# A graph layer on one core: 200 instead of 192 binned groups, summed in blocks of 32, 16 and 8

## The chip, the cores and the metric

The kernel runs on one core of a Trainium2 chip. The metric is the device time in microseconds (us), from the first to the last instruction of the core. Engines: TensorE (PE), VectorE (DVE), ScalarE (ACT), GpSimd (POOL), and SyncE (SP), which issues most transfers.

## What is computed

A layer of a graph network over 6250 nodes and 206,250 edges; `dst` is sorted, `src` is not.

```python
h = maximum(layernorm(x), 0)                       # 6250 x 64
m = relu(concat([h[dst], edge_attr]) @ W1.T + b1)  # 206250 x 128
m = relu(m @ W2.T + b2)                            # 206250 x 128
agg = segment_sum(m, src) / maximum(count(src), 1) # 6250 x 128
z = relu(concat([h, agg, u]) @ Wa.T + ba)
out = x + z @ Wb.T + bb                            # 6250 x 64
```

## The kernel before, in words

**Tiling.** The edges go through in 403 groups of 512 (four tiles of 128). All five engines run the same software pipeline of steps s = 0, 1, 2, ...; each engine has its own instruction stream in the order of the code, and semaphores tie them. For group s the first layer is one float32 product of 512 columns (two instructions, L1373); a window of 64 table rows stands for `h[dst] @ W1`, since `dst` is sorted. ACT evacuates it with relu (L923), PE multiplies by W2 one step later (L1399, 8 instructions for four tiles), ACT evacuates that (L943).

**Two ways to sum by `src`.** A *plain* group is summed within each tile by a mask product (L1389), copied by ACT (L931) into one of four buffers `scat`, and added to four tables in DRAM by four indirect transfers of GpSimd (L821, one for each tile). DVE makes the mask (L1182) and the row numbers (L1187, L1190). ACT has to wait until the transfers from a buffer have landed before it fills it again, so PE can run ahead of GpSimd by four plain groups at most.

A *binned* group (every odd group from 3 to 385, 192 in all) needs no scatter of its own. Node n belongs to bin n % 49: 49 bins of 128 nodes. DVE ranks each row within its bin (L1154 to L1163, after a product with `prefix`, L1417) and makes a permutation with 4 places in each of 49 bins and 60 places for overflow. PE permutes the four tiles (L1350, 16 instructions), ACT copies them (L906, four copies of 128x260), and SP stores them to `slots` in DRAM (L606, L607). The 60 overflow rows of the four tiles are added by DVE (L1204, L1205) into `vpre`; SP copies `vpre` of each group into one half of `V` (L615), two groups fill one `V`, and PE makes of V's key column a row (L1410), DVE a mask, PE a sum (L1423), and GpSimd one scatter for each pair of groups (L809).

**Blocks and units.** When the 32 binned groups of a block are in `slots`, the block is summed in 25 *units* of two bins (the last has one). For a unit SP issues two loads (L629), each 128 rows (32 groups x 4 places) of 520 floats (4 tiles x 130). DVE compares the keys with 128 node numbers (L1215, 8 one-hots for a unit), PE multiplies (L1361, 16 instructions), DVE adds the result to `acc` (L1134; L1131 copies for the first block). Three units fit in the ring of buffers `BR`.

`unit_steps` writes the order by hand. The 25 units of a block are spread over the steps until the next block is complete, always on even steps: one unit in about 2.56 steps, 0.78 a pair of steps (0.83 for the fifth block, 60 steps). The last block starts 5 steps after its last group, group 385. From group 386 on all groups are plain, and the units of the last block go beside them, two in a step after the third.

**SP's stream** in each step: the edge block (L579, every second step), the `dst` rows (L587, every fourth), the row number of the window and its load (L592, L593), the `src` rows (L599), then for a group six steps back the two stores (L606, L607), for one seven steps back the copy to V (L615), then the loads of the step's unit. The copy is issued in the step after the one in which PE wants it in the program's count, so SP runs ahead of PE.

**The end.** After the last load SP waits for all scatters and reads the four tables (L645, L641); DVE adds them and `acc` (L1231 to L1234), ACT scales, PE transposes and multiplies by Wa and Wb, in 13 chunks.

A *pair* below is two steps, one plain and one binned group: 4 + 1/2 scatters. The lines that set the share of binned groups and the order of the units:

```python
LAST_SORTED = 386
def is_sorted(g): return 2 < g < LAST_SORTED and g % 2 == 1
firsts = [block[-1] + VREAD + 2 for block in BLOCKS[:-1]] + [BLOCKS[-1][-1] + TAIL_LAG]
s = firsts[k] + 2 * (span * q // (2 * UNITS))
```

Of the kernel before, what the change touches and what calls it, by code (L numbers as in the profile page):

```python
# [47 lines left out]
LAST_SORTED = 386  # L48
# [16 lines left out]
ROUNDS = [[(0, 4), (4, 5)]] + [[(a, a + 4), (a + 4, a + 8)] for a in range(5, 45, 8)] + [[(45, 49)]]  # L65
# [26 lines left out]
BLOCKS = [BINNED[k:k + BLOCK] for k in range(0, NH, BLOCK)]  # L92
# [42 lines left out]
def unit_steps():  # L135
    at = {}
    firsts = [block[-1] + VREAD + 2 for block in BLOCKS[:-1]] + [BLOCKS[-1][-1] + TAIL_LAG]
    for k in range(len(BLOCKS) - 1):
        for q in range(UNITS):
            span = firsts[k + 1] - firsts[k]  # L140
            s = firsts[k] + 2 * (span * q // (2 * UNITS))
            at.setdefault(s, []).append((k, q))
    alone = VSUM - TAIL_LAG
    for q in range(UNITS):
        s = firsts[-1] + (q if q < alone else alone + (q - alone) // 2)
        at.setdefault(s, []).append((len(BLOCKS) - 1, q))
    return at
# [3 lines left out]
STEPS = max(max(UNITS_AT) + TAIL_LEAD + 1, NG + VSUM + 1)  # L151
# [32 lines left out]
def arrived(m):  # L184
    parts = {n: unit_bins(q)[1] for (_, q), n in UNIT_NO.items()}
    return sum(parts[n] for n in users(m))


# [1338 lines left out]
```

## Time and profile before

| what | value |
|---|---|
| median of 3 timed runs | 1929.52 us (1921.0 to 1935.98) |
| span of the profiled execution | 1917.2 us |
| PE busy | 1737.8 us (91%) |
| GpSimd busy | 1528.8 us (80%) |
| ACT busy | 1433.6 us (75%) |
| DVE busy | 1289.0 us (67%) |
| PE weight loads busy | 1470.5 us (77%) |
| TensorE clock granted, mean | 0.972 of full speed |
| DMA traffic, mean | 194 GB/s |

The profiled execution gives the span from the first to the last instruction, and its times are those of one execution; the timed runs are executions without the profiler. SP computes nothing, so it has no busy time on the page: its issues and waits stand in the timeline and in a view of waits of their own. "Issue" ahead of an instruction is idle time for which the profile shows no other engine.

### The profile page before, as it was taken

What the parts mean: (1) busy time and instruction counts of PE and PEld (TensorE: products, weight loads), DVE (VectorE), ACT (ScalarE), POOL (GpSimd) and SP (SyncE); (2) the same over time, 40 slices, a digit from 0 to 9 for tenths busy, and PEclk for the clock granted to TensorE, in tenths of its full rate; (3) what the DMA queues carried; (4) which work ended last, traced back from release to release, by engine and by line L of the source; (5) the groups of instructions that cost most, each with busy time, mean ns of one, the idle gap of its engine ahead of it and who ended that gap; (6) DMA issues with size and microseconds to landing.
All of it is one profiled execution on the core that took longest, in us unless ns stands there. A gap on an engine that the chain in (4) does not pass through costs nothing.

```text
span 1917.2 us, 43265 instructions
## 1 busy us (share of the span) xinstructions
PE 1737.8 (91%) x12472; PEld 1470.5 (77%) x12472; DVE 1289.0 (67%) x4235; ACT 1433.6 (75%) x2975; POOL 1528.8 (80%) x991
## 2 busy tenths in 40 slices
PE   6898888999999999999999999999999999978837
PEld 4677666888888888888788788888888888867725
DVE  8565555667767676777776777777776676756727
ACT  4788887878888877788788787878877877862306
POOL 8488888888888888888888888888888888888850
PEclk8999999999999999999999999999999999998969
DMA  9988888999999999999999999999999999999856
GB/s 329 269 166 151 151 151 149 187 198 193 198 192 192 201 190 196 201 192 192 200 197 187 185 199 198 200 193 197 204 194 198 191 199 199 197 183 234 176 116 217
DMA packets 319400, 372.10 MB, mean 194 GB/s; under 512 B 42272, under 2 KB 203264, under 8 KB 318528
## 3 DMA queue, kind: packets, MB, share of 16 engines
q1 hardware_dynamic: 182400, 305.12, 55.6%
q0 software_dynamic: 135360, 62.15, 34.4%
q8 instruction: 110, 1.80, 0.4%
q10 hardware_dynamic: 1408, 2.03, 0.3%
q14 instruction: 122, 1.00, 0.1%
HBM read 203.87 MB, written 159.27 MB: 189 GB/s over the span
## 4 chain that ended last, share of the span: by engine, by line
POOL 44%; issue 19%; PE 17%; DMA 11%; DVE 5%; ACT 3%; SPq 1%; ACTq 0%; POOLq 0%; DVEq 0%
POOL sums L821 39%; DMA sums<-regA,idx 7%; POOL sums L809 5%; PE bank L1361 4%; PE bank L1350 4%; PE bank L1399 3%; PE bank L1373 3%; DVE regC L1215 2%; PE bank L1389 1%; DMA regC<-slots 1%; DMA regA<-sums 1%; DMA sums<-vscat,vidx 1%; ACT regA L931 1%; DVE regC L1182 1%; PE bank L1275 1%
## 5 line engine op out<-in xcount | busy, mean ns | idle before, releaser
L821 POOL DMA_INDIRECT sums<-regA,idx x844 | 1333.9, 1580 | 291.7 <-issue 244.4
L1350 PEld LDWEIGHTS bank<-h,regC 128*128 128x128 f32 x3072 | 389.0, 194 | 183.1 <-ACT h L943 134.0
L1350 PE MATMUL bank<-h,regC 128*128 128x130 f32 x3072 | 421.7, 281 | 63.0 <-ACT h L943 62.8
L1373 PE MATMUL bank<-regA,L 128*128 128x512 f32 x806 | 435.8, 623 | 4.6 <-DVE regA L1147 3.0
L1399 PE MATMUL bank<-w,h 128*128 128x128 f32 x3224 | 431.3, 277 | 0.0
L923 ACT ACTIVATE h<-bank,b1c 128x512 f32<-128x512 f32 x403 | 275.7, 684 | 198.0 <-PE bank L1373 193.1
L1399 PEld LDWEIGHTS bank<-w,h 128*128 128x128 f32 x3224 | 398.0, 194 | 1.1 <-ACT h L923 0.6
L1215 DVE TENSOR_SCALAR regC<-lows,regC 128x128 f32<-128x128 f32 x1176 | 257.7, 315 | 147.6 <-DMA regC<-slots 124.0
L1361 PE MATMUL bank<-regC 128*128 128x129 f32 x2352 | 298.3, 281 | 34.4 <-issue 19.0
L943 ACT ACTIVATE h<-bank 128x512 f32<-128x512 f32 x403 | 240.9, 598 | 111.1 <-PE bank L1399 107.2
L1361 PEld LDWEIGHTS bank<-regC 128*128 128x128 f32 x2352 | 277.2, 193 | 41.8 <-issue 38.1
L1389 PEld LDWEIGHTS bank<-h,regC 128*128 128x128 f32 x1688 | 223.1, 192 | 102.2 <-issue 98.7
L906 ACT ACTIVATE regC<-bank 128x260 f32<-128x260 f32 x768 | 270.4, 385 | 4.5 <-PE bank L1350 3.9
L912 ACT ACTIVATE bank<-b2b 128x512 f32<-128x512 f32 x403 | 242.4, 602 | 11.2
L1389 PE MATMUL bank<-h,regC 128*128 128x130 f32 x1688 | 224.7, 276 | 0.5 <-ACT h L943 0.5
L1182 DVE TENSOR_TENSOR regC<-src,srcF 128x512 f32<-128x512 uint16 x211 | 146.4, 694 | 99.7 <-DMA src<-rows_src 95.1
L1156 DVE TENSOR_TENSOR regC<-bank,ranks 128x784 f32<-128x784 f32 x192 | 184.5, 961 | 0.0
L931 ACT ACTIVATE regA<-bank 128x520 f32<-128x520 f32 x211 | 126.4, 599 | 71.7 <-DMA sums<-regA,idx 54.6
L809 POOL DMA_INDIRECT sums<-vscat,vidx x96 | 153.0, 1594 | 31.2 <-issue 26.8
L1154 DVE TENSOR_REDUCE rank<-bank 128x4 f32<-128x196 f32 x192 | 68.3, 356 | 140.0 <-PE bank L1417 137.6
L1140 DVE TENSOR_TENSOR regC<-bank,overs 128x240 f32<-128x240 f32 x192 | 77.0, 401 | 115.8 <-PE bank L1434 114.9
L954 ACT ACTIVATE regA<-dstR,oh_bias 64x512 f32<-64x512 uint8 x192 | 137.6, 717 | 4.9
(142 smaller groups left out, 1540.3 us busy)
## 6 DMA issues: line engine op xcount, KB each, us to landing
regC<-slots SPq DMA_DIRECT2D x294, 260.0 KB, 5.6
regA<-in_ea SPq DMA_DIRECT2D x202, 256.0 KB
slots<-regC SPq DMA_DIRECT2D x192, 260.0 KB
src<-rows_src SPq DMA_DIRECT2D x107, 256.0 KB
slots<-regC SPq DMA_DIRECT2D x192, 138.1 KB
sums<-regA,idx POOLq DMA_INDIRECT x844
dstR<-rows_dst SPq DMA_DIRECT2D x101, 128.0 KB
sums<-zeros SPq DMA_DIRECT2D x20, 645.0 KB, 7.0
```

The costliest lines, as they stand in the source:

```text
L809: nc.gpsimd.indirect_dma_start(out=sums[k], out_offset=bass.IndirectOffsetOnAxis(ap=vidx[:, j % 6:j % 6 + 1], axis=0), in_=vscat[:, j % 4, ...
L821: nc.gpsimd.indirect_dma_start(out=sums[k], out_offset=bass.IndirectOffsetOnAxis(ap=idx[:, n % RING, t:t + 1], axis=0), in_=scat[:, n % 4, ...
L906: nc.scalar.activation(slot_sb[:, n % 2, :, t, :], psSlot(t), ACT.Copy).then_inc(slot_ready, 1)
L912: nc.scalar.activation(psL2(g % 2).rearrange("p (t f) -> p t f", t=TPG), b2b[:, :].unsqueeze(1).broadcast_to([P, TPG, H]), ACT.Copy).then_ ...
L923: nc.scalar.activation(h1[:, s % 2, :], psL1(s % 2), ACT.Relu, bias=b1c[:, :]).then_inc(h1_ready, 1)
L943: nc.scalar.activation(h2[:, g % 2, :, 0:H], psL2(g % 2).rearrange("p (t f) -> p t f", t=TPG), ACT.Relu).then_inc(h2_ready, 1)
L1215: made = VE.tensor_scalar(oh2[0:rows, m % 2, i, t, :], lows[0:rows, i, :], loaded(m)[0:rows, i, t, C:W], -float(b), ALU.subtract, ALU.is_e ...
L1350: last = T.matmul(psSlot(t)[:, k, :], place, h2[:, g % 2, t, :], start=True, stop=True)
L1361: last = T.matmul(psUnit(m)[:, i * C:(i + 1) * C], oh2[0:rows, m % 2, i, t, :] if not general else zeros[0:rows, 0:LO], loaded(m)[0:rows, ...
L1373: T.matmul(psL1(s % 2), L[:, s % RING, :], R[:, s % RING, :], start=True, stop=True).then_inc(l1_done, 1)
L1389: last = T.matmul(bank[:, 6 + t // 2, (t % 2) * W:(t % 2 + 1) * W], S[:, n % 4, t, :], h2[:, g % 2, t, :], start=True, stop=True)
L1399: last = T.matmul(psL2(g % 2)[:, t * H:(t + 1) * H], h1[:, g % 2, t * TILE:(t + 1) * TILE], w2[:, :], start=False, stop=True, skip_group_c ...
```

## The change

- Every odd group from 3 to 401 is binned: 200 binned groups and 203 plain ones (before 192 and 211).
- The blocks have 32, 32, 32, 32, 16, 16, 16, 16 and 8 groups. For a block of 16 or 8 a load puts two or four times as many rows on the partitions, each with two tiles or one tile of the four (`FOLD` 2 or 4): it still fills 128 partitions, with rows of 260 or 130 floats. A unit then has 4 or 2 one-hots instead of 8, and 8 or 4 matmul instructions instead of 16; it still has two loads and one addition.
- The units of blocks 0 to 2 are spread as before. From block 3 on they stand as soon as the schedule allows: every second step for block 3 (steps 266 to 315), one in each step for blocks 4 to 7 (316 to 415), two in a step for block 8 (416 to 428). The last step that has a group is 402.
- The ring `BR` is counted in quarters: three units of block 3, six of blocks 4 to 7 or twelve of block 8 fit. The three spare buffers of the last block are gone. From step 405 on the units' sums go through four banks of PSUM.
- DVE writes the overflow of the first group of a pair straight into V; SP copies only the second (one copy a pair of groups).
- V's key row is made by PE's transpose instead of a product with the identity.
- ACT copies the permuted tiles in pairs: two copies of 128x520 a group.
- The count of overflows at the start covers 800 tile columns instead of 784, with one part more.

```diff
-LAST_SORTED = 386
+FIRST_SORTED, LAST_SORTED = 3, 402
-BLOCK = 32
+SIZES = [32] * 4 + [16] * 4 + [8]
-ROUNDS = [[(0, 4), (4, 5)]] + [[(a, a + 4), (a + 4, a + 8)] for a in range(5, 45, 8)] + [[(45, 49)]]
+ROUNDS = [[(0, 4), (4, 5)]] + [[(a, a + 4), (a + 4, a + 8)] for a in range(5, 45, 8)] + [[(45, 49), (49, 50)]]
-UNIT_RING, SPARE = 3, 3
-TAIL_LAG, TAIL_LEAD = 5, 1
+UNIT_RING = 3
+LATE, LATE_LAG, STEADY = 2, 5, 3
-BLOCKS = [BINNED[k:k + BLOCK] for k in range(0, NH, BLOCK)]
+BLOCKS = [BINNED[sum(SIZES[:k]):sum(SIZES[:k + 1])] for k in range(len(SIZES))]
+FOLD = [max(SIZES) // len(block) for block in BLOCKS]
 def unit_steps():
...
+    due = 4 * firsts[STEADY]
+    for k in range(STEADY, len(BLOCKS)):
+        due = max(due, 4 * firsts[k])
+        for q in range(UNITS):
+            at.setdefault(due // 4, []).append((k, q))
+            due += 8 // FOLD[k]
...
-            return bank[:, 0 if m >= PAIRED and m % 2 else 1, 0:PAIR * C]
+            return bank[:, 1 if m < ALONE else 2 + (m - ALONE) % 4, 0:PAIR * C]
...
-                if is_sorted(s - VREAD):
-                    n = BINNED_NO[s - VREAD]
-                    j, half = n // 2, n % 2
-                    sp.wait_ge(vpre_ready, n + 1)
-                    if half == 0:
-                        wait(sp, vsum_done, j - 1)
-                        wait(sp, vidx_ready, j - 1)
-                    sp.dma_start(V[half * OVER:(half + 1) * OVER, j % 2, :], vpre[:, half, :]).then_inc(v_in[n % 4], 16)
+                if closes(s - VREAD):
+                    j = BINNED_NO[s - VREAD] // 2
+                    sp.wait_ge(vpre_ready, 2 * j + 2)
+                    sp.dma_start(V[OVER:2 * OVER, j % 2, :], vpre[:, :]).then_inc(v_in[j % 2], 16)
...
-                    if buffer_of(m) >= UNIT_RING:
-                        sp.wait_ge(vpre_ready, NH)
-                    if len(users(m)) > 1:
-                        sp.wait_ge(unit_done, users(m)[-2] + 1)
-                    h0 = BINNED_NO[block[0]]
+                    wait(sp, unit_done, UNIT_FREED[m])
+                    h0, n = BINNED_NO[block[0]], len(block)
+                    folded = slots.rearrange("n p (f x) -> n (p f) x", f=FOLD[k])
+                    rows = CAP * FOLD[k]
                     for i in range(nb):
-                        sp.dma_start(loaded(m)[0:CAP * len(block), i, :, :].rearrange("p t c -> p (t c)"),
-                                     slots[h0:h0 + len(block), CAP * (b + i):CAP * (b + i + 1), :]).then_inc(unit_in[buffer_of(m)], 16)
+                        sp.dma_start(loaded(m)[0:rows * n, i, :, :].rearrange("p t c -> p (t c)"),
+                                     folded[h0:h0 + n, rows * (b + i):rows * (b + i + 1), :]).then_inc(unit_in[UNIT_AT[m]], 16)
...
-                nc.scalar.activation(slot_sb[:, n % 2, :, t, :], psSlot(t), ACT.Copy).then_inc(slot_ready, 1)
+                nc.scalar.activation(slot_sb[:, n % 2, :, t:t + 2, :].rearrange("p h t c -> p t h c"), psSlots, ACT.Copy).then_inc(slot_ready, 1)
...
-                    if n >= 2:
-                        dve.wait_ge(v_in[(n - 2) % 4], 16 * ((n - 2) // 4 + 1))
+                    j, half = n // 2, n % 2
+                    if half == 0:
+                        wait(dve, vsum_done, j - 1)
+                        wait(dve, vidx_ready, j - 1)
+                    elif j >= 1:
+                        dve.wait_ge(v_in[(j - 1) % 2], 16 * ((j - 1) // 2 + 1))
...
-                    VE.tensor_tensor(vpre[:, n % 2, :], vhalf[:, 0, :], vhalf[:, 1, :], ALU.add).then_inc(vpre_ready, 1)
+                    VE.tensor_tensor(V[0:OVER, j % 2, :] if half == 0 else vpre[:, :], vhalf[:, 0, :], vhalf[:, 1, :], ALU.add).then_inc(vpre_ready, 1)
...
-                        for t in range(TPG):
+                        for t in range(size):
...
-                if t >= 2:
-                    pe.wait_ge(slot_ready, TPG * n + t - 1)
+                if t == 2:
+                    pe.wait_ge(slot_ready, 2 * n + 1)
...
-                    T.matmul(psVrow, V[:, j % 2, C:W].broadcast_to([P, P]), ident[:, :], start=True, stop=True).then_inc(vrow_done, 1)
+                    T.transpose(psVrow, V[:, j % 2, C:W].broadcast_to([P, P]), ident[:, :]).then_inc(vrow_done, 1)
```

SP's stream in a late pair of steps, where the fifth block was summed before and a block of 16 is now. `p_table` is the window's load, `V<-vpre` the copy, `regC<-slots` the loads of a unit, `slots<-regC` the stores. Before:

```order
L593 DMA L<-p_table 64x128
L615 DMA V<-vpre 60x130
L629 DMA regC<-slots 128x1x520 x2
L592 TENSOR_LOAD base
L592 ISA x2
L593 ISA
L593 DMA L<-p_table 64x128
L606 DMA slots<-regC 68x520
L607 DMA slots<-regC 128x520
L579 DMA regA<-in_ea 64x1024
```

And now:

```order
L605 DMA L<-p_table 64x128
L611 DMA src<-rows_src 128x1024
L623 DMA V<-vpre 60x130
L636 DMA regC<-slots 128x1x260 x2
L604 TENSOR_LOAD base
L604 ISA x2
L605 ISA
L605 DMA L<-p_table 64x128
L618 DMA slots<-regC 68x520
L619 DMA slots<-regC 128x520
L636 DMA regC<-slots 128x1x260 x2
L591 DMA regA<-in_ea 64x1024
```

Each of the two steps has a unit's two loads now, with rows half as long, and the copy to V stands in every second pair only.

SP's stream at the end, from the last window's load to the reads of the tables (`regA<-sums`). Before:

```order
L593 DMA L<-p_table 64x128
L629 DMA regC<-slots 128x1x520 x11
L645 DMA regA<-sums 128x516 x4
L641 DMA regA<-sums 128x1032 x16
```

And now:

```order
L618 DMA slots<-regC 68x520
L619 DMA slots<-regC 128x520
L636 DMA regC<-slots 128x1x260 x2
L623 DMA V<-vpre 60x130
L636 DMA regC<-slots 128x1x260 x17
L636 DMA regC<-slots 128x1x130 x49
L652 DMA regA<-sums 128x516 x4
L648 DMA regA<-sums 128x1032 x16
```

After the last window's load 11 loads were left; now 78 are (10 more stand ahead of this piece), 49 of them those of block 8, and the reads stand behind them all.

DVE's stream in the step in which it also makes the permutation, in the same late stretch. `A` and `V`, `vpre` are the last rows of the permutation's work, `regC<-lows` the one-hots, `regB<-regB,bank` the addition to `acc`, `regC<-bank,overs` the next step's first row. Before:

```order
L1175 TENSOR_TENSOR A<-binF,bins 128x196
L1204 TENSOR_TENSOR vhalf<-regC 60x260
L1205 TENSOR_TENSOR vpre<-vhalf 60x130
L1140 TENSOR_TENSOR regC<-bank,overs 128x4x60
L1147 TENSOR_SCALAR regA<-dstR,oh_row 64x512
```

And now:

```order
L1180 TENSOR_TENSOR A<-binF,bins 128x196
L1213 TENSOR_TENSOR vhalf<-regC 60x260
L1214 TENSOR_TENSOR V<-vhalf 60x130
L1139 TENSOR_TENSOR regB<-regB,bank 128x258
L1224 TENSOR_SCALAR regC<-lows,regC 128x128 x4
L1145 TENSOR_TENSOR regC<-bank,overs 128x4x60
```

An addition and four one-hots stand in this step too, where none stood before.

## Rows read from the trace of the kernel before

**Rows 1.** The page: busy time, and the chain that ended last, by engine.

```profile
PE 1737.8 (91%) x12472; PEld 1470.5 (77%) x12472; DVE 1289.0 (67%) x4235; ACT 1433.6 (75%) x2975; POOL 1528.8 (80%) x991
...
POOL 44%; issue 19%; PE 17%; DMA 11%; DVE 5%; ACT 3%; SPq 1%; ACTq 0%; POOLq 0%; DVEq 0%
```

**Rows 2.** Line L821: by group (busy, mean | idle, releaser), then least/median/most ns.

```profile
L821 POOL DMA_INDIRECT sums<-regA,idx x844 | 1333.9, 1580 | 291.7 <-issue 244.4
...
L821 POOL DMA_INDIRECT sums<-regA,idx x844: 1543/1545/4717, 69.1 to 1853.9; - x169
```

**Rows 3.** Line L923, one a step: first and last start, whole and in three stretches.

```profile
L923 ACT ACTIVATE h<-bank,b1c x403: 669/687/691, 56.9 to 1818.8; 128x512 f32<-128x512 f32 x135
...
L923 ACT ACTIVATE h<-bank,b1c x65: 670/687/690, 113.5 to 383.3; 128x512 f32<-128x512 f32 x65
...
L923 ACT ACTIVATE h<-bank,b1c x255: 669/688/691, 386.6 to 1479.2; 128x512 f32<-128x512 f32 x128
...
L923 ACT ACTIVATE h<-bank,b1c x48: 670/688/691, 1484.4 to 1688.1; 128x512 f32<-128x512 f32 x48
```

**Rows 4.** All waits of SP's queue from 1484 to 1694 us: total, times, longest.

```profile
SPq L592 <- PE bank L1373: 4.7, 10, 0.8
SPq L579 <- PE bank L1373: 4.3, 4, 2.0
SPq L615 <- DVE vpre L1205: 3.2, 6, 0.8
SPq L606 <- ACT regC L906: 2.7, 8, 0.6
SPq L629 <- PE bank L1361: 1.5, 3, 0.7
```

**Rows 5.** Timeline of SP from 1568 us: start, duration, issue.

```profile
1568.51 0.51 SPq L606 DMA_DIRECT2D slots<-regC  x1
1569.07 0.35 SPq L607 DMA_DIRECT2D slots<-regC  x1
1569.46 0.50 SPq L579 DMA_DIRECT2D regA<-in_ea  x1
1571.47 0.50 SPq L593 DMA_DIRECT2D L<-p_table  x1
1572.09 0.92 SPq L615 DMA_DIRECT2D V<-vpre  x1
1573.06 1.25 SPq L629 DMA_DIRECT2D regC<-slots  x2
```

**Rows 6.** Timeline of PE from 1569 us, and its weight loads' busy time from 1484 to 1694.

```profile
1569.49 1.10 PE L1373 MATMUL bank<-regA,L 128*128 128x512 f32 x2
1570.43 1.06 PE L1389 MATMUL bank<-h,regC 128*128 128x130 f32 x8
1571.32 1.05 PE L1399 MATMUL bank<-w,h 128*128 128x128 f32 x8
...
1484.00:1694.00 210.00, 200.50 (x1488) 172.78 (x1488) 146.06 (x507) 167.54 (x349) 174.37 (x112) 1.00 0.95 196
```

**Rows 7.** DVE at a unit: its waits for loads, then two rows of the timeline.

```profile
  DMA regC<-slots: 124.0, 91
...
1766.16 0.76 DVE L1134 TENSOR_TENSOR regB<-regB,bank 128x258 f32<-128x258 f32 x2
...
1768.86 3.48 DVE L1215 TENSOR_SCALAR regC<-lows,regC 128x128 f32<-128x128 f32 x16 [1.95 <-PE bank L1361]
```

**Rows 8.** Timeline of the end: last scatter, first reads of the tables, DVE's first addition.

```profile
1853.86 1.54 POOL L821 DMA_INDIRECT sums<-regA,idx  x1 [0.30 <-issue]
1857.22 1.88 SPq L645 DMA_DIRECT2D regA<-sums  x4
...
1862.34 1.23 DVE L1231 TENSOR_TENSOR regC<-regA 128x1032 f32<-128x1032 f32 x1 [31.21 <-DMA regA<-sums]
```

**Rows 9.** The page: two forms of ACT's copies out of PSUM.

```profile
L906 ACT ACTIVATE regC<-bank 128x260 f32<-128x260 f32 x768 | 270.4, 385 | 4.5 <-PE bank L1350 3.9
...
L931 ACT ACTIVATE regA<-bank 128x520 f32<-128x520 f32 x211 | 126.4, 599 | 71.7 <-DMA sums<-regA,idx 54.6
```

More of the change, by code:

```diff
@@ L136, in unit_steps @@
     at = {}
-    firsts = [block[-1] + VREAD + 2 for block in BLOCKS[:-1]] + [BLOCKS[-1][-1] + TAIL_LAG]
-    for k in range(len(BLOCKS) - 1):
+    late = len(BLOCKS) - LATE
+    firsts = [block[-1] + (VREAD + 2 if k < late else LATE_LAG) for k, block in enumerate(BLOCKS)]
+    for k in range(STEADY):
         for q in range(UNITS):
             span = firsts[k + 1] - firsts[k]
[L141 to L146, printed above, removed]
+            at.setdefault(firsts[k] + 2 * (span * q // (2 * UNITS)), []).append((k, q))
+    due = 4 * firsts[STEADY]
[4 more added lines that the diff above has]
+            due += 8 // FOLD[k]
     return at
 UNITS_AT = unit_steps()
-STEPS = max(max(UNITS_AT) + TAIL_LEAD + 1, NG + VSUM + 1)
+STEPS = max(max(UNITS_AT) + 2, NG + VSUM + 1)
 CONSTS = 16
@@ L176, in added_for, with load_steps, ring_table @@
-def added_for(m):
-    return m if m <= PAIRED else m - 1
+UNIT_OF = {n: kq for kq, n in UNIT_NO.items()}
+APART = NG + 2
+ALONE = sum(len(units) for s, units in UNITS_AT.items() if s < APART)
+def load_steps():
+    at = {}
+    for s, units in sorted(UNITS_AT.items()):
+        for k, q in units:
+            at.setdefault(s + (1 if k >= len(BLOCKS) - LATE else 0), []).append((k, q))
+    return at
+LOADS_AT = load_steps()
+QUARTERS = UNIT_RING * TPG
+def ring_table():
+    place, freed, arrived, at = {}, {}, {}, 0
+    last, begun = {}, [0] * QUARTERS
+    for m in range(len(UNIT_OF)):
+        k, q = UNIT_OF[m]
+        size = TPG // FOLD[k]
+        mine = range(at, at + size)
+        place[m] = at
+        freed[m] = max((last[c] + 1 for c in mine if c in last), default=0)
+        for c in mine:
+            last[c] = m
+        begun[at] += unit_bins(q)[1]
+        arrived[m] = begun[at]
+        at = (at + size) % QUARTERS
+    return place, freed, arrived
@@ L180, in units_until @@
 def units_until(s):
     return sum(len(u) for at, u in UNITS_AT.items() if at <= s)
[L184 to L186 removed]
 def unit_bins(q):
     return PAIR * q, min(PAIR, NBIN - PAIR * q)
[L193 to L194 removed]
+UNIT_AT, UNIT_FREED, UNIT_ARRIVED = ring_table()
@@ L197, in build @@
+assert LO * NBIN == NKEPT >= N and OVER + PLACES == PW and 2 * OVER <= P and NH == 2 * NV and NG + max(VSUM, VLAG) < STEPS and NH == sum(SIZES)
+assert NBIN == BA * BA and PACK * BA <= P and NS == NPACK * PACK and PARTS[-1][1] == NPACK and (FIRST_SORTED - 1) * TPG + 2 * NS <= NT and all(len(units) == 1 for s, units in UNITS_AT.items() if s < APART)
 def build(nc, x, src_cols, dst_cols, src_rows, dst_rows, ea, u, w1t, b1, w2t, b2, wat, ba, wbt, bb, out):
@@ L467, in build @@
         slot_out = [sem(f"slot_out{k}") for k in range(2)]
-        v_in = [sem(f"v_in{k}") for k in range(4)]
+        v_in = [sem(f"v_in{k}") for k in range(2)]
         earlier_ready = sem("earlier_ready")
@@ L476, in build @@
         vscat_ready = sem("vscat_ready")
-        unit_in = [sem(f"unit_in{k}") for k in range(UNIT_RING + SPARE)]
+        unit_in = [sem(f"unit_in{k}") for k in range(QUARTERS)]
         oh2_ready = sem("oh2_ready")
```

73 lines of the change are left out of this document (29 added, 44 removed).

## The prediction

> **What bounds the kernel now.** I read the page first, then the scatters, the rate of the steps by stretch, SP's waits, and the spacing on PE. The page says PE 91% busy, but the chain that ended last is GpSimd's: 44%, and 19% "issue" [rows 1]. The scatters explain it: one takes 1.580 us and the idle "issue" time before it is 244.4 / 844 = 0.29, so one leaves each 1.87 us, from 69.1 to 1853.9 us [rows 2]. A pair of steps has 4.5 of them: 8.42 us. The steps go at that rate: from step 16 to step 80, 32 pairs, (383.3 - 113.5) / 32 = 8.43 us a pair, when almost no unit is summed; with units it is (1479.2 - 386.6) / 127 = 8.60, and in the fifth block (1688.1 - 1484.4) / 23.5 = 8.67 [rows 3]. GpSimd is the bound. Two streams stand close behind it, and the reader should see them before counting any gain.
>
> The first is SP. From 1484 to 1694 us its waits sum to 16.4 us [rows 4], 8% of 210. The other 92%, 7.99 us of each pair, it issues. The timeline shows what [rows 5]: the issues follow each other at 0.04 us, a unit's two loads take 1.25 (0.64 each with the gap), the copy to V 0.92 (0.96), the second store 0.35 (0.39), and between the edge block's end at 1569.96 and the window's load at 1571.47 stands the reading of the row number.
>
> The second is PE. Eight instructions of 128 columns start 0.89 us apart from the next eight (0.111 each), two of 512 columns take 0.94 [rows 6]. A pair has 16 + 16 + 8 such instructions for the groups, 16 x 0.83 = 13.3 for units and 2 for V: 55.3 x 0.111 = 6.14; the first layer adds 1.88 and the three small bf16 products I put at 0.15. Sum 8.17 of 8.67.
>
> The Trainium skill ("Perfetto Trace Analysis", Identifying the Most-Contended Engine) says that matmul busy time is a bad measure and weight-load busy time a good one. By that rule PE would have 18% to spare, since its weight loads are busy 172.8 of 210 us [rows 6]; the spacing of the same rows leaves 6%. By the rule the term for block 3 below would be 6 us smaller; I go by the spacing.
>
> **The change, part by part.**
>
> *Eight groups from plain to binned.* 8 x 4 = 32 scatters go, 4 come: 28 x 1.87 = 52.4 us less for GpSimd, whose last scatter ended at 1855.4 [rows 8]. It could end at 1803.0. PE gets 8 x (16 - 8) instructions more, 7 us in all.
>
> *Steps up to 266.* Units come as before. SP loses half a copy to V a pair, 0.48, and goes from about 7.93 to 7.45 us. I expect its lead to grow and the rate to fall between GpSimd's own 8.43 and today's 8.60; I take 8.48. DVE now has V's first half to write and waits there for a product of V that stands one step earlier on PE, ahead of the rank DVE has already waited for: nothing. The transpose takes one instruction instead of two, 0.11 us in two pairs at best, and PE waits for the same copy as before. ACT's four copies of 0.385 become two like the 128x520 form of 0.599 [rows 9], 0.34 less a pair on an engine with slack; PE's third tile now waits for both first tiles, but 0.89 us of second-layer products stand between. Both at nothing; at the outside 0.1 us a pair either way.
>
> *Block 3, steps 266 to 315.* One unit a pair instead of 0.83: PE needs 0.17 x 1.78 more, less the transpose: 8.4. With the 0.3 us of small stalls that PE has anyway, 8.7.
>
> *Blocks 4 to 7, steps 316 to 402: 43 pairs.* Here is the main cost. Folding halves the bytes of a load, not their number: four loads a pair instead of 1.66. SP: 7.99 - 0.48 - 1.66 x 0.64 + 4 x 0.64 = 9.01 us a pair, above GpSimd's 8.43. With the few waits that stay, 9.15. The price of a load with shorter rows is not in the trace. Below it lies the second store (0.39), above it the copy to V (0.96), whose rows have 520 bytes; I take the same line's 0.64. The bounds give 8.0 (then PE's 8.4 to 8.6 decides) and 10.3. PE needs the same 16 instructions a pair for units. DVE gets 0.385 us of one-hots more and 1.17 additions of 0.38 [rows 7], 0.8 us on 146.06 of 210 us busy [rows 6]: 6.9 of 9.15, beside SP.
>
> The Trainium skill ("Perfetto Trace Analysis", What "DMA-bound" means) has a kernel bound by the DMA sequencer when the issuing engine's track is solid, and says that large descriptors then matter. The 92% of rows 4 agree. By that rule folding is the wrong direction on SP, and the sum would be the one I make.
>
> So step 402 comes at 383.3 (step 80, rows 3) + 93 x 8.48 + 25 x 8.7 + 43 x 9.15 = 1782.9 us; before it came at 1818.8 [rows 3]: 35.9 earlier. GpSimd, at most four groups behind as before (1855.4 - 1818.8 = 36.6), ends at 1803 or soon after and is no longer late.
>
> *The end.* Before, the last units lay beside plain groups and were hidden: PE and DVE were done long before the last scatter, DVE then stood idle 31.21 us for the tables [rows 8]. Now 11 units of half size and 25 of a quarter stand behind the last group. DVE: a half unit 4 x 0.218 + 0.38 (3.48 / 16, 0.76 / 2, rows 7) + 0.15 to pass semaphores = 1.4 us, a quarter unit 1.0. SP: each quarter unit still two loads, 1.28. SP is slower. Step 404 ends one pair after step 402, at 1791.4. The first load of block 8 needs the place of the unit of step 410, 6 units on: 1799.8. Then 49 x 0.64 = 31.4: 1831.2. The four reads of the tables follow at once, and DVE could start 5.1 us after the first of them was issued (1862.34 - 1857.22, rows 8): 1836.3, about when the last unit is added too. From there to the end it was 1917.2 - 1862.34 = 54.9 us, unchanged: the DVE pipeline of 13 chunks. PE's products for the first chunks, which were done early before, now come in that phase; DVE stays ahead of them by a chunk: nothing.
>
> Span 1836.3 + 54.9 = 1891.2, 26 us less than 1917.2. The larger count at the start (2% more columns, one part more) I put at under 1 us. The profiled span lies 12.3 us below the median of the runs, 1929.5; I keep that distance: 1904. Of the 52.4 us that GpSimd is spared, half comes out.
>
> **The rivals.**
>
> *A. SP's issue gets shorter with the rows, and GpSimd stays the bound.* For it: SP's issues do differ (0.35 to 0.96). Against: they don't follow the bytes, since the shortest row list (V) is the dearest. At 0.39 a load, PE sets blocks 4 to 7 at 8.6; step 402 would come at 1757, but GpSimd, four groups behind, allows 1803.0 - 36.6 = 1766.4. Then 8.5 + 11 x 1.4 + 25 x 1.0 = 48.9 of DVE: 1815.3; span 1871, time 1883.
>
> *B. The gain is given back.* DVE executes in order and waits for loads: 124.0 us for 147 units today [rows 7], 0.84 each, now hidden under GpSimd. With a unit in each step and SP late, these come onto the path: two a pair, 1.68, against 0.66 today: 43 x 1.02 = 44 us if all of it shows, 22 if half. Time 1926 to 1948; I take 1930, no change. Against it: DVE still has 2 us of slack a pair.
>
> *C. Slower.* A load with short rows costs what the copy to V costs, 0.96, since rows of 520 bytes are what block 8 has too. Blocks 4 to 7 go at 10.3: 43 x 1.15 = 49 us more; block 8 at 49 x 0.96 adds 16. Time 1969. It decides from about 0.83 a load (45 us more than my sum). For it: no other row shows rows of that size. Against: the V copy has 60 partitions and goes from one on-chip place to another; the unit's loads come from DRAM.
>
> *D. The change does not do what it says.* PE and SP with their small waits, not GpSimd, would already set 8.60, and neither fewer scatters nor SP's half copy brings anything before step 266: 93 x 0.12 = 11 us more than my sum, 1915. Against: GpSimd's idle time besides "issue" is 47 us in all [rows 2], about half of it the start.
>
> **Chances.** My forecast 0.50, A 0.22, B 0.14, C 0.07, D 0.07. The time is 1904. Its own range is 1892 to 1918 (8.45 or 8.6 before step 266 is 14 us, 9.0 or 9.3 after 316 is 13, the tail's issue cost 5). The full range reaches to A below and into B above: 1879 to 1938. About 1% (19 us) is what a measurement of this kernel can tell from no change: faster by more (below 1910) 0.35 of my forecast's 0.50 and all of A: 0.57; within it 0.15 + B's 0.11 + D's 0.06 = 0.32; slower 0.11.
>
> **What would show it.** Right: the pair takes under 8.55 us up to step 266 and SP's waits grow there; above step 316 it is about 9.15, with SP's waits near nothing and GpSimd idle between scatters; a load of 260 floats issues in 0.60; the last scatter ends by 1810; SP issues block 8 without a gap and the tables' reads follow; DVE starts its first chunk near 1836. Wrong: a pair above 316 at 8.5 (A) or, with SP waiting too, at 9.7 or more and DVE waiting for `regC<-slots` (B); loads of 0.9 us (C); the pair at 8.6 before step 266 with GpSimd idle (D). A tail above 60 us from the last first-layer copy to DVE's first chunk would upset the last term.

## The result, and the profile after: 31 us slower

The changed kernel takes 1956.32 us (median of 4 runs, 1953.31 to 1960.1), the kernel before beside it 1925.26 (4 runs, 1920.66 to 1935.98): a ratio of 1.0156, interval 1.0124 to 1.0187. The forecast was 1904. The profiled execution has a span of 1958.3 us where before had 1917.2. The table ahead of the prediction gives 1929.52 for before; a fourth run is in the 1925.26.

The page of the kernel after, its busy times and its chain:

```profile
PE 1781.5 (91%) x12576; PEld 1505.1 (77%) x12576; DVE 1338.5 (68%) x4408; ACT 1450.6 (74%) x2626; POOL 1481.0 (76%) x963
...
POOL 38%; PE 34%; issue 15%; DMA 6%; ACT 4%; DVE 3%; POOLq 0%; SPq 0%; ACTq 0%; DVEq 0%
...
L1370 PE MATMUL bank<-regC 128*128 128x129 f32 x2450 | 335.8, 288 | 74.5 <-ACT vscat L970 58.2
```

The shares in the first line are within a point or so of before's [rows 1], except GpSimd's, which fell from 80% to 76%. What is new stands in the other two. PE's share of the chain went from 17% to 34%, and the unit products, L1370 (L1361 before), now have 58.2 us of idle time in front of them with a releaser that my prediction never names: `vscat`, ACT's copy of the V sum.

The step rates tell where. The first-layer copy on line L930 (L923 before, as [rows 3]), one a step, whole and in three stretches, each row with the start of its first and its last instruction:

```profile
L930 ACT ACTIVATE h<-bank,b1c x403: 667/687/692, 60.7 to 1842.8; 128x512 f32<-128x512 f32 x135
...
L930 ACT ACTIVATE h<-bank,b1c x186: 667/687/692, 384.9 to 1169.3; 128x512 f32<-128x512 f32 x186
...
L930 ACT ACTIVATE h<-bank,b1c x50: 668/687/692, 1174.8 to 1384.0; 128x512 f32<-128x512 f32 x50
...
L930 ACT ACTIVATE h<-bank,b1c x87: 670/687/692, 1389.3 to 1842.8; 128x512 f32<-128x512 f32 x87
```

Step 316 starts at 1389.3 us; my sum had 1389.4. From there to step 402 a pair takes (1842.8 - 1389.3) / 43 = 10.55 us, against 8.67 in the fifth block of before [rows 3] and 9.15 in my sum. That is 60 us more than forecast, and the result is 52 us above the forecast. One stretch holds the error.

The last rows of GpSimd, SP and DVE, as [rows 8] and [rows 2] (the scatter is L828 now):

```profile
L828 POOL DMA_INDIRECT sums<-regA,idx x812: 1543/1545/3857, 69.4 to 1865.6; - x163
...
1852.24 43.89 SPq L636 DMA_DIRECT2D regC<-slots  x66
...
1896.66 1.80 SPq L652 DMA_DIRECT2D regA<-sums  x4
...
1900.52 1.23 DVE L1240 TENSOR_TENSOR regC<-regA 128x1032 f32<-128x1032 f32 x1 [0.47 <-DMA regA<-sums]
```

The scatters are fewer, 812 for 844, but the last starts at 1865.6, not at 1853.9: they went as the groups came. And DVE's idle time before its first chunk fell from 31.21 to 0.47 us, because the last units now stand there.

Of the waits between steps 316 and 402 (1389 to 1843 us) the largest six: engine, line, releaser, total us, times, longest.

```profile
ACT h L930 <- PE bank L1382: 96.0, 64, 3.9
POOL sums L816 <- ACT vscat L970: 77.8, 18, 6.1
DVE regC L1145 <- PE bank L1443: 71.6, 39, 4.4
PEld bank L1370 <- ACT vscat L970: 61.7, 22, 2.9
PE bank L1370 <- ACT vscat L970: 57.4, 22, 2.7
DVE regB L1139 <- PE bank L1370: 44.2, 22, 2.6
```

In before's whole trace PE's wait for `vscat` is this:

```profile
PE bank L1361 <- ACT vscat L965: 0.4, 1, 0.4
```

PE and GpSimd wait for ACT's copy, ACT and DVE wait for PE. PE's stops are 22, one in four steps of that stretch, of 2.6 us each. One such stop on the timeline, 1712 to 1722 us (start, duration, engine and line, idle time before it and its releaser in brackets; SP and the rest of DVE and ACT left out):

```profile
1712.83 0.41 PE L1432 MATMUL bank<-V,vS 128*128 128x129 f32 x2
...
1713.57 0.72 ACT L959 ACTIVATE regA<-dstR,oh_bias 64x512 f32<-64x512 uint8 x1
...
1714.31 0.60 ACT L919 ACTIVATE bank<-b2b 128x512 f32<-128x512 f32 x1
...
1714.94 0.63 ACT L964 ACTIVATE regA<-regA 64x512 f32<-64x512 f32 x1
...
1715.59 0.28 ACT L970 ACTIVATE vscat<-bank 128x129 f32<-128x129 f32 x1
...
1715.92 2.09 PE L1370 MATMUL bank<-regC 128*128 128x129 f32 x8 [2.68 <-ACT vscat L970]
...
1716.64 1.56 POOL L816 DMA_INDIRECT sums<-vscat,vidx  x1 [3.76 <-ACT vscat L970]
...
1717.80 1.92 PE L1382 MATMUL bank<-regA,L 128*128 128x512 f32 x2
```

PE finished the V sum (L1432) at 1713.24. Next in its order is the unit of the same step. Both write bank 1 of PSUM (`psVsum` and `psUnit` are columns of it), so the code lets the unit start only when ACT has copied the V sum out. ACT's step has that copy last, behind two one-hot passes and a seed: 0.72 + 0.60 + 0.63 = 1.95 us of work that has nothing to do with it. The rule that the code keeps is the one in the Trainium skill, "PSUM — Partial Sum Buffer", PSUM bank collisions raise a hardware error: two engines may not use one bank at once on the same partitions, not even in different columns. No run here shows a collision; they show what the wait costs.

The second thing in these rows is PE after the stop. Eight unit products took 2.09 us, and two first-layer products 1.92. A few us earlier in the same trace they took:

```profile
1708.03 1.13 PE L1370 MATMUL bank<-regC 128*128 128x129 f32 x8
...
1709.05 1.10 PE L1382 MATMUL bank<-regA,L 128*128 128x512 f32 x2
```

The granted clock beside them: in stretches before, during and after this stop, then in the 5.1 us behind two later stops of the same length, then over blocks 3 and 4 to 7 (us; busy time of PE, PEld, DVE, ACT, POOL; PE clock; DMA share; GB/s):

```profile
1708.00:1712.00 4.00, 3.97 (x30) 3.51 (x31) 3.33 (x13) 2.58 (x6) 3.39 (x3) 1.00 1.07 234
1713.20:1715.90 2.70, 0.04 (x1) 0.00 (x0) 2.20 (x7) 2.57 (x5) 0.00 (x0) 0.87 0.91 174
1715.90:1721.00 5.10, 5.08 (x17) 4.05 (x18) 1.21 (x5) 0.69 (x1) 3.75 (x3) 0.50 0.70 155
...
1739.01:1744.11 5.10, 5.10 (x25) 4.07 (x26) 1.21 (x5) 1.17 (x2) 3.77 (x3) 0.67 0.62 139
...
1760.81:1765.91 5.10, 5.10 (x37) 4.37 (x38) 1.53 (x6) 2.59 (x5) 3.76 (x3) 1.00 0.72 149
...
1174.00:1389.00 215.00, 214.44 (x1610) 186.69 (x1609) 160.92 (x568) 173.92 (x314) 179.08 (x115) 1.00 0.97 207
1389.00:1843.00 454.00, 394.93 (x2754) 339.29 (x2753) 295.38 (x1027) 302.28 (x538) 315.34 (x201) 0.94 0.84 169
```

PE idles for 2.7 us and then runs the next 5 us at 0.50, the lower of its two levels (1.2 GHz of 2.4). Not every stop does this: of the 22 in this stretch, 11 are followed by 5.1 us below 1.00 (4 at 0.50, 7 at 0.67 to 0.72) and 11 by 5.1 us at 1.00, though 21 of the 22 are the same 2.68 us long. Over the stretch the mean clock is 0.94, which by an estimate is 0.06 x 454 = 27 us lost. PE's busy time puts it at 22: 394.93 us here against 372.77 for the same products in e5 below, at a clock of 1.00. With the 57.4 us of waiting that is 79 to 85 us, or 1.8 to 2.0 a pair. That is the step from about 8.6 to 10.55.

### The profile page after: what moved, and what is told of

It reads as the page before. It is cut to its first block, busy times and chain, and to the rows that moved or that the text cites. A ratio compares the mean times of both kernels' runs of the same rounds, so it can differ in the third digit from the quotient of the medians.

```text
span 1958.3 us, 43507 instructions
## 1 busy us (share of the span) xinstructions
PE 1781.5 (91%) x12576; PEld 1505.1 (77%) x12576; DVE 1338.5 (68%) x4408; ACT 1450.6 (74%) x2626; POOL 1481.0 (76%) x963
## 4 chain that ended last, share of the span: by engine, by line
POOL 38%; PE 34%; issue 15%; DMA 6%; ACT 4%; DVE 3%; POOLq 0%; SPq 0%; ACTq 0%; DVEq 0%
POOL sums L828 33%; PE bank L1370 8%; PE bank L1359 7%; PE bank L1408 6%; PE bank L1382 6%; DMA sums<-regA,idx 4%; POOL sums L816 4%; PE bank L1398 3%; DMA sums<-vscat,vidx 1%; ACT regA L964 1%; ACT regA L959 1%; DVE regC L1071 1%; ACT regA L938 1%; ACT h L930 0%; ACT vscat L970 0%
## 5 line engine op out<-in xcount | busy, mean ns | idle before, releaser
L828 POOL DMA_INDIRECT sums<-regA,idx x812 | 1283.0, 1580 | 274.9 <-issue 239.2
L1359 PEld LDWEIGHTS bank<-h,regC 128*128 128x128 f32 x3200 | 403.7, 192 | 176.8 <-ACT h L949 117.2
L1359 PE MATMUL bank<-h,regC 128*128 128x130 f32 x3200 | 449.0, 284 | 59.0 <-ACT h L949 58.8
L1382 PE MATMUL bank<-regA,L 128*128 128x512 f32 x806 | 441.9, 631 | 2.6 <-DVE regA L1152 2.4
L1370 PE MATMUL bank<-regC 128*128 128x129 f32 x2450 | 335.8, 288 | 74.5 <-ACT vscat L970 58.2
L930 ACT ACTIVATE h<-bank,b1c 128x512 f32<-128x512 f32 x403 | 275.8, 684 | 172.4 <-PE bank L1382 167.8
L1370 PEld LDWEIGHTS bank<-regC 128*128 128x128 f32 x2450 | 304.4, 199 | 96.0 <-ACT vscat L970 74.2
L913 ACT ACTIVATE regC<-bank 128x520 f32<-128x520 f32 x400 | 241.6, 604 | 93.4 <-PE bank L1359 91.0
L1398 PEld LDWEIGHTS bank<-h,regC 128*128 128x128 f32 x1624 | 216.0, 194 | 106.4 <-issue 97.2
L1224 DVE TENSOR_SCALAR regC<-lows,regC 128x128 f32<-128x128 f32 x1225 | 268.6, 305 | 14.3 <-DMA regC<-slots 12.3
L816 POOL DMA_INDIRECT sums<-vscat,vidx x100 | 156.1, 1561 | 109.2 <-ACT vscat L970 77.8
L1398 PE MATMUL bank<-h,regC 128*128 128x130 f32 x1624 | 219.2, 278 | 0.6 <-ACT h L949 0.6
L1161 DVE TENSOR_TENSOR regC<-bank,ranks 128x784 f32<-128x784 f32 x200 | 192.5, 963 | 0.1
L938 ACT ACTIVATE regA<-bank 128x520 f32<-128x520 f32 x203 | 121.3, 597 | 42.3 <-DMA sums<-regA,idx 29.4
L959 ACT ACTIVATE regA<-dstR,oh_bias 64x512 f32<-64x512 uint8 x200 | 143.4, 717 | 5.1
```

What stands on the lines that cost most here:

```text
L816: nc.gpsimd.indirect_dma_start(out=sums[k], out_offset=bass.IndirectOffsetOnAxis(ap=vidx[:, j % 6:j % 6 + 1], axis=0), in_=vscat[:, j % 4, ...
L828: nc.gpsimd.indirect_dma_start(out=sums[k], out_offset=bass.IndirectOffsetOnAxis(ap=idx[:, n % RING, t:t + 1], axis=0), in_=scat[:, n % 4, ...
L913: nc.scalar.activation(slot_sb[:, n % 2, :, t:t + 2, :].rearrange("p h t c -> p t h c"), psSlots, ACT.Copy).then_inc(slot_ready, 1)
L930: nc.scalar.activation(h1[:, s % 2, :], psL1(s % 2), ACT.Relu, bias=b1c[:, :]).then_inc(h1_ready, 1)
L1224: made = VE.tensor_scalar(oh2[0:rows, m % 2, i, t, :], lows[0:rows, i, :], loaded(m)[0:rows, i, t, C:W], -float(b), ALU.subtract, ALU.is_e ...
L1359: last = T.matmul(psSlot(t)[:, k, :], place, h2[:, g % 2, t, :], start=True, stop=True)
```

## The experiments

My theory, W: units every step bring unit products and V sums together on PE, and PE then waits for ACT's last copy. Its rivals: S, SP's four loads a pair (the forecast's own mechanism, only dearer than it was priced); and the small edits (V's half without a copy, the transpose, ACT's copies in pairs). All kernels below compute the whole result.

### e1: ACT copies the V sum earlier

The change with one block of ACT's step moved up, from its end to right behind the second pair of slot copies:

```
                     evac_slots(s - 2, 1)
+                if closes(s - VSUM):
+                    ...
+                    nc.scalar.activation(vscat[:, j % 4, :], psVsum, ACT.Copy).then_inc(vscat_ready, 1)
 ...
-                if closes(s - VSUM):
-                    ...
-                    nc.scalar.activation(vscat[:, j % 4, :], psVsum, ACT.Copy).then_inc(vscat_ready, 1)
```

> The changed kernel with ACT's copy of the V sum (vscat) made right after the second pair of permuted tiles, ahead of three other ACT instructions (two of the next one-hot, one seed, 1.95 us together). Theory W (the unit's products wait for that copy, because both lie in one PSUM bank, and a unit in every step meets it in one step of four): the wait of 2.7 us shrinks to about 0.7, the pair from step 316 to 402 falls from 10.5 us to 8.9 to 9.4, the time to 1890 to 1915. Rival S (SP's stream of four loads a pair sets those steps): nothing of this touches SP, the pair stays above 10.2 and the time within 1950 to 1962.

Measured: 1919.03 us (10 runs, 1912.93 to 1923.88), ratio to before 0.9947 (0.9923 to 0.9971). The whole loss went with one moved block: 1.0156 became 0.9947. Its steps from 316, the windows row of that stretch, the two largest of SP's waits in it, and two waits that say who is late:

```profile
L930 ACT ACTIVATE h<-bank,b1c x87: 669/687/691, 1387.9 to 1798.6; 128x512 f32<-128x512 f32 x87
```

```profile
1387.00:1799.00 412.00, 378.57 (x2761) 324.34 (x2761) 297.13 (x1030) 302.91 (x539) 316.95 (x202) 1.00 0.92 186
```

```profile
SPq L618 <- ACT regC L913: 6.5, 6, 3.8
...
SPq L604 <- PE bank L1382: 5.7, 14, 0.7
...
DVE regC L1224 <- DMA regC<-slots: 58.7, 53, 4.6
...
PE bank L1370 <- DVE regB L1139: 20.7, 24, 3.5
```

The clock is back at 1.00 and the pair at (1798.6 - 1387.9) / 43 = 9.55 us. I expected 8.9 to 9.4 and a time of 1890 to 1915, so both came out a little above. The SP rows say why: all its waits sum to 20.1 of 412 us, 5%, so 9.1 us of each pair are issue time. DVE now waits for the units' loads, 58.7 us in this stretch against 12.3 in the whole run of the changed kernel, and PE waits for DVE's additions. With the stop gone SP is what is late, as the forecast had it, at 9.55 and not 9.15. PE still waits for `vscat` here, 11.3 us in 22 times, 0.5 a time, and none of these short waits is followed by a lower clock.

### e2: no unit where a V sum stands

The change with the copy left in place and the planner passing over such steps:

```
         for q in range(UNITS):
+            if due // 4 < NG + VSUM and closes(due // 4 - VSUM):
+                due += 4
             at.setdefault(due // 4, []).append((k, q))
```

> The changed kernel with no unit in a step that has the V sum (one step in four) as long as there are such steps: three half-size units in four steps from step 316 on, so more units remain behind the last group. Theory W: no wait for the copy up to step 402, the pair there at 8.5 to 8.8 us, step 402 at 1755 to 1770; the tail has 55 units instead of 36 and takes about 80 us instead of 58; the time 1890 to 1910. Rival S: three loads a pair instead of four save at most 0.64 us, the pair at 9.8 or above, and with the longer tail the time does not fall below 1945.

Measured: 1911.47 us (8 runs, 1908.42 to 1921.59), ratio 0.9913 (0.9886 to 0.9941). Its steps from 316 and its scatters:

```profile
L932 ACT ACTIVATE h<-bank,b1c x87: 669/687/692, 1390.5 to 1762.6; 128x512 f32<-128x512 f32 x87
...
L830 POOL DMA_INDIRECT sums<-regA,idx x812: 1544/1546/4875, 69.4 to 1792.8; - x163
```

A pair takes (1762.6 - 1390.5) / 43 = 8.65 us, the rate of before, and as W had it; the time is 1.5 us above what W gave, and far from the 1945 or more of S alone. But it changes two things at once: no unit meets a V sum, and only three units are loaded in four steps, one load a pair less, which spares SP 0.64 us of it. So it rules out S alone, and does not say how much of its gain is the load. The units pushed back stand at the end: from step 402 to DVE's first chunk 89 us pass (1762.6 to 1851.4), where before had 43.5; I had expected about 80.

### e3: the same meeting, made in the kernel before

If W is right, the kernel before can be spoiled by one number, with its loads per pair as they are:

```
-            at.setdefault(firsts[k] + 2 * (span * q // (2 * UNITS)), []).append((k, q))
+            at.setdefault(firsts[k] + 2 * (span * q // (2 * UNITS)) + 1, []).append((k, q))
```

> The kernel before with the units of its first five blocks one step later, on odd steps, where every second odd step has the V sum: 0.39 meetings a pair of steps. Work, loads and SP's stream are the same. Theory W: each meeting costs what it costs in the changed kernel, about 3.9 us with the slower clock behind it, 1.0 to 1.5 us a pair between steps 74 and 386: 2060 to 2160 us. Rival S, and any theory of loads: no change, 1915 to 1940.

Measured: 2092.05 us in its one run, against a median of 1928.56 for the kernel before in 17 runs on the same chip (1917.7 to 1938.34); one run gives no interval, but 163 us lie far outside that spread, and I had expected 2060 to 2160. Two of its waits from 364 to 1780 us, then its steps from 364.9 us on and the clock there:

```profile
PE bank L1361 <- ACT vscat L965: 133.0, 54, 2.5
...
POOL sums L809 <- ACT vscat L965: 145.9, 44, 4.9
```

```profile
L923 ACT ACTIVATE h<-bank,b1c x292: 669/680/690, 364.9 to 1775.5; 128x512 f32<-128x512 f32 x146
...
364.00:1780.00 1416.00, 1268.08 (x8966) 1094.36 (x8965) 898.36 (x3066) 1023.05 (x2118) 1066.02 (x664) 0.95 0.86 174
```

PE's wait is 0.4 us in before and 133.0 here. It is the cleanest of the runs: same loads, same blocks, no small edits, and the same signature (2.5 us a stop, clock 0.95, GpSimd waiting behind). The shift also moves the units' loads, one-hots and additions into odd steps, on SP and DVE; but in that stretch PE waits for nothing of theirs, and its only other wait there, 14.8 us for ACT's `h`, was 25.4 in before over the same 364 to 1780 us. A pair takes (1775.5 - 364.9) / 145.5 = 9.69, 1.1 more than 8.60. It also shows that before was fast by a parity: V sums stand in every second odd step, its units in even ones.

### e4 and e7: the small edits alone

e4 is the kernel before with V's first half written by DVE in place, the key row by transpose, and slot copies in pairs; its core:

```
-                    VE.tensor_tensor(vpre[:, n % 2, :], vhalf[:, 0, :], vhalf[:, 1, :], ALU.add).then_inc(vpre_ready, 1)
+                    VE.tensor_tensor(V[0:OVER, j % 2, :] if half == 0 else vpre[:, :], vhalf[:, 0, :], vhalf[:, 1, :], ALU.add).then_inc(vpre_ready, 1)
 ...
-                nc.scalar.activation(slot_sb[:, n % 2, :, t, :], psSlot(t), ACT.Copy).then_inc(slot_ready, 1)
+                nc.scalar.activation(slot_sb[:, n % 2, :, t:t + 2, :].rearrange("p h t c -> p t h c"), psSlots, ACT.Copy).then_inc(slot_ready, 1)
```

e7 is e4 without the second of these (ACT copies the tiles one by one again) and the waits that go with it.

> The kernel before with the small edits alone: overflow of the first group straight into V and one copy a pair by SP, V's key row by transpose, ACT's copies of permuted tiles in pairs. If these explain the faster pair of the changed kernel up to step 266 (8.50 instead of 8.60): 8.45 to 8.55 a pair from step 74 to 330, more in the fifth block (8.9 to 8.6), time 1900 to 1918. If they do nothing and the difference was chance: 1920 to 1932.

> The kernel of e4_small_edits with ACT's copies of the permuted tiles one by one again: only the overflow straight into V, one copy a pair by SP, and the transpose remain. If SP's half copy (0.48 us a pair) is what makes the steps of e4 faster: 1905 to 1915, as e4. If ACT's pairs do it: 1922 to 1932, as before.

Measured: e4 1909.31 us (4 runs, 1904.92 to 1910.69), ratio 0.9884 (0.9839 to 0.9928); e7 1912.97 (9 runs, 1904.91 to 1916.96), ratio 0.9918 (0.9892 to 0.9944). The small edits are not what makes the kernel slower; together they gain 1.2% by the ratio, 19 us by the medians, and the copy that SP is spared and the transpose alone gain 0.8%, 12 us by the medians. Whether ACT's pairs add anything the two intervals do not tell. e4's steps over the whole run:

```profile
L921 ACT ACTIVATE h<-bank,b1c x403: 667/687/691, 57.2 to 1806.0; 128x512 f32<-128x512 f32 x135
```

Step 402 comes at 1806.0 where before had 1818.8 [rows 3]: a rate gain in blocks that GpSimd was said to bound. In e7 it comes at 1808.4.

### e5 and e6: SP relieved, with and without the moved copy

S is tested by taking loads from SP. From block 4 on the second load of a unit is issued by ACT, three steps ahead; the first five units of block 7 stay with SP:

```
+                        if i == 1 and (k, q) in SHARED:
+                            continue
 ...
+                for k, q in ACT_LOADS_AT.get(s, ()):
+                    ...
+                    wait(act, unit_done, UNIT_FREED[m])
+                    act.dma_start(loaded(m)[0:rows * n, 1, :, :]..., folded[h0:h0 + n, ...]).then_inc(unit_in[UNIT_AT[m]], 16)
```

e6 is the change with this, e5 is e1 with this.

> The changed kernel with the same sharing of loads, but with the copy of the V sum where the change has it. Theory W then S: the wait for the copy still sets the steps, the pair stays at 10.0 to 10.8 from step 316 to 402 (ACT has two issues a pair more ahead of its work, so rather more than less), and only the tail gains 8 to 12 us: 1942 to 1956. Rival S alone (SP's four loads set the pair of the changed kernel): 8.9 or less a pair, 1880 to 1900.

> The kernel of e1_copy_first with the second load of each unit of blocks 4 to 8 issued by ACT three steps ahead instead of by SP (all but the first five of block 7). With the wait for the V sum's copy mostly gone, theory S says that SP's four loads a pair set the 9.1 to 9.6 us of e1 from step 316 to 391 (its waits there are 14 of 390 us): with two of them gone the pair falls to 8.5 to 8.9, step 402 comes at 1762 to 1775 instead of 1799, and the tail, 59 us there, falls to 46 to 52, since DVE sets it with 1.0 a quarter unit instead of SP with 1.3: 1870 to 1890 us. Rival W2 (what is left of the wait for the copy, and DVE, set e1's pair): the pair stays at 9.2 or above, only the tail gains, 1905 to 1912.

Measured: e6 1948.88 us (1945.21 to 1950.92), ratio 1.0114 (1.0068 to 1.016); e5 1888.27 us (4 runs, 1886.33 to 1892.25), ratio 0.9803 (0.9757 to 0.9849). PE's wait in e6, from 1387 to 1835 us:

```profile
PE bank L1396 <- ACT vscat L984: 57.5, 22, 2.7
```

Alone, relief for SP is worth little: 7 us by the medians, with intervals that overlap, and a pair of (1834.5 - 1387.8) / 43 = 10.39 for 10.55, since PE's 22 stops remain as they were (57.5 us for 57.4). Behind the moved copy it is worth 28 to 31 us (by the ratios, 0.9947 and 0.9803; by the medians, 1919.03 and 1888.27). The two bounds stand one behind the other: the wait first, SP next. e5's steps from 316, SP's largest wait there, the windows row, the scatters and DVE's first chunk:

```profile
L944 ACT ACTIVATE h<-bank,b1c x87: 687/687/692, 1389.8 to 1775.3; 128x512 f32<-128x512 f32 x87
...
L842 POOL DMA_INDIRECT sums<-regA,idx x812: 1543/1545/3296, 70.0 to 1798.2; - x163
```

```profile
SPq L630 <- ACT regC L927: 26.1, 19, 4.5
```

```profile
1389.00:1776.00 387.00, 372.77 (x2762) 323.02 (x2761) 296.83 (x1030) 300.76 (x539) 320.00 (x202) 1.00 0.96 199
...
1827.60 1.23 DVE L1266 TENSOR_TENSOR regC<-regA 128x1032 f32<-128x1032 f32 x1 [1.07 <-DMA regA<-sums]
```

A pair takes (1775.3 - 1389.8) / 43 = 8.97 us, just above the 8.5 to 8.9 that I expected (the time was within 1870 to 1890), PE is 96% busy, and SP now has time to wait for ACT. It is the fastest of the kernels run, faster than before and after both.

### e8: what the eight groups are worth

e5 with 192 binned groups in `[32] * 4 + [16] * 4` as before, the last round cut to fit and everything else of it kept:

```
-FIRST_SORTED, LAST_SORTED = 3, 402
+FIRST_SORTED, LAST_SORTED = 3, 386
-SIZES = [32] * 4 + [16] * 4 + [8]
+SIZES = [32] * 4 + [16] * 4
```

> The kernel of e5_share_copy_first with 192 binned groups as before (blocks of 32 x 4 and 16 x 4, the last 17 groups plain); the count at the start covers 768 tile columns. Theory G (with the waits gone the 28 scatters fewer are what is left of the change's gain): GpSimd is the bound again to its last scatter at 1842 to 1852, the units of the last block are hidden, 1903 to 1914 us, as e4_small_edits, against 1888 of e5. Rival U (the freed wait and the shared loads are the gain, not the groups): 1885 to 1895, as e5.

Measured: 1915.74 us (5 runs, 1914.15 to 1923.08), ratio to before 0.9927 (0.9887 to 0.9967), against e5's 0.9803; 2 us above the range of theory G, and far from rival U. The eight groups bring 24 us by the ratios and 27 by the medians, once nothing else is in the way. Its scatters:

```profile
L842 POOL DMA_INDIRECT sums<-regA,idx x844: 1543/1545/4773, 69.2 to 1849.3; - x169
```

The last scatter starts 51.1 us later than e5's (1849.3 to 1798.2), which is the 28 x 1.87 = 52.4 of the forecast, met to 1.3 us. About half of it shows in the time, because the last units no longer lie beside plain groups: from the start of the last scatter to DVE's first chunk 8.4 us pass in e8 (1849.3 to 1857.7) and 29.4 in e5 (1798.2 to 1827.6).

## Why the prediction was wrong

The forecast summed the span as 1891.2; it was 1958.3. To get the time it added the 12.3 us by which before's profiled span lay below the median; here the span lies 2.0 above it (1958.3 and 1956.32), so the time was missed by only 52.3. The 67.1 us too few in the span, term by term:

**Steps up to 266: right.** Forecast at 1171.9 us, measured at 1174.8; the pair took (1169.3 - 384.9) / 92.5 = 8.48 for 8.48. The sign named for it came too: SP's waits from 386 to 1170 us sum to 87.9 us, 54.7 in before. Part of the credit stays open, though. The small edits alone gained 1.2% in e4, in the fifth block too. The forecast priced only the half copy and put the transpose and ACT's pairs at nothing; e4 and e7 do not tell the half copy from the transpose.

**Block 3: right.** (1389.3 - 1174.8) / 25 = 8.58 for 8.7, with PE busy 214.44 of 215 us there, so PE set the pair as forecast. That step 316 came 0.1 us from its forecast is partly luck: 2.9 us too late up to step 266, 3.0 too fast here.

**Blocks 4 to 7: the step that failed.** "SP: ... 9.01 us a pair ... With the few waits that stay, 9.15" was 10.55, or 60 us over 43 pairs. SP's issue time was right: four loads a pair, and its queue without the waits is (454 - 66.5) / 43 = 9.01 us a pair, to the hundredth the forecast's sum; in the end phase 66 loads took 43.89 us, 0.665 each for the 0.64 taken. What failed is "with the few waits that stay", and the sentence "PE needs the same 16 instructions a pair for units". I priced the move of units into odd steps by the number of instructions and by SP's queue, and did not ask what stands beside them in an odd step on PE. There the V sum stands, and the unit waits for a copy that is last in ACT's order. It cost 57.4 us of waiting and, with a clock of 0.94, 22 to 27 us of slower work. e1 removes it by the copy's place, e2 by the unit's; e3 makes it in the kernel before; e6 shows that SP was not late while it lasted. With it gone SP's bound is at 9.55 (e1), 0.4 a pair above the sum: "the few waits that stay" were priced at 0.14 a pair and are 20.1 / 43 = 0.47 there.

**GpSimd's 52.4 us: right as a term, hidden in the result.** e5 against e8 shows 51.1 us between their last scatters. In the changed kernel GpSimd waited 77.8 us for the same `vscat` between steps 316 and 402 and began its last scatter at 1865.6, where the forecast had the last one end at 1803.0.

**The end: nearly right.** Step 402 to DVE's first chunk was 57.7 us (1842.8 to 1900.52) for 53.4 forecast (1782.9 to 1836.3); the load's 0.665 for 0.64 explains 49 x 0.025 = 1.2 of the 4.3. From the first chunk to the end 57.8 passed for 54.9; no run was made to say why. In e5 the first of these is 52.3. The forecast's warning mark of 60 us was not reached.

**The rivals.** A (loads that issue faster) fell: the median of the folded units' loads is 598 ns. B (DVE waits for loads) had the right time for its upper end, 1948, but not the mechanism: DVE waited 12.3 us for unit loads in the whole run, less than before's 124.0 and not 44 more. Only in e1, with the stops gone, do such waits come onto the path, 58.7 us above step 316. C (0.96 us a load) fell with the same 598 ns, though its 10.3 us a pair and its time of 1969 lay nearest to what was measured; that was luck, since no load was dear. D (nothing comes out before step 266) fell: the pair went from 8.60 to 8.48 there. None of the four held what happened, and 1956 lay above the range. Two small slips in the rivals change no chance: A's step 402 sums to 1759 and not 1757, and before has 150 units and not 147 (294 loads; the last unit of a block has one load). SP's "waits near nothing above 316" failed too: all of them sum to 66.5 of 454 us in the changed kernel, the most of it in the row below, against 20.1 of 412 in e1, where the mechanism I had forecast is at work.

```profile
SPq L618 <- ACT regC L913: 53.9, 21, 5.6
```

The trace of before could have shown it. The wait `PE bank L1361 <- ACT vscat L965: 0.4, 1, 0.4` was there, small because of where units stood. The question to it was what becomes of a guard when the thing it guards moves by one step.

e5's pair is 8.97 and not the 8.6 of block 3: PE is busy 372.77 / 43 = 8.67 of it, and it waits 11.8 us for `vscat` (22 times) and 1.8 for DVE in that stretch, 0.32 a pair. What stays open: why some stops of the same length are followed by a lower clock and others are not, and how much of e4's gain is the transpose and how much SP's copy; neither was tried alone.

## What to carry to other kernels

When a change moves work by a step in an in-order queue, list what else stands in the step it moves to and which guards the two share; a wait of 0.4 us in the old trace can be one that the old order happened to avoid. Where two producers share a PSUM bank, the consumer that frees it belongs at the front of its engine's step: here moving one copy of 0.28 us ahead of 1.95 us of other work was worth 37 us (1956.32 to 1919.03). And a stop of PE can cost twice, once as idle time and again as a lower clock behind it: here behind 11 of 22.

## What the runs showed of the hardware that I had not expected

**A stop of 2.7 us can be followed by 5 us at the lower clock, and need not be.** Behind the stop that ended at 1715.9 us the granted clock was 0.50 until 1721.0, and eight products of 129 columns took 2.09 us instead of 1.13; behind the equally long stop that ended at 1760.8 it was 1.00. In the changed kernel 11 of 22 stops were followed by a clock below 1.00, in e3 45 of 54 stops of 2.46 us, in e1 none of 22 waits of up to 0.64 us. Over the 22 stops the loss by the clock (22 to 27 us) came to nearly half of the stops themselves (57.4 us).

**SP's price for a load does not follow its bytes.** The loads of units in the changed kernel in three stretches: up to 1389 us with whole tiles (260.0 KB a load), from 1400 to 1840 us with half tiles, and from 1850 us on with half and quarter tiles (line, count: least, median and most ns, first and last start):

```profile
L636 SPq DMA_DIRECT2D regC<-slots x202: 549/603/1587, 345.3 to 1386.9; - x101
...
L636 SPq DMA_DIRECT2D regC<-slots x163: 534/598/1991, 1401.0 to 1836.2; - x163
...
L636 SPq DMA_DIRECT2D regC<-slots x68: 514/575/1112, 1849.6 to 1895.6; - x68
```

Medians of 603, 598 and 575 ns: a folded unit costs SP almost what a whole one does. A block of 16 groups has as many units as one of 32, so for the same groups the issue time doubles.
